# Written-out step loops, and attention's output sent to its rows from ScalarE's queue

## The reference

```python
q = (x @ wq).reshape(b, n, H, DH).transpose(0, 2, 1, 3)      # k and v alike; n = 1024, H = 16, DH = 16
sim = jnp.einsum('bhid,bhjd->bhij', _fq(q, dq, 128.0, 8), _fq(k, dk, 128.0, 8)) * SCALE
attn = jax.nn.softmax(sim, axis=-1)
out = jnp.einsum('bhij,bhjd->bhid', _fq(attn, dw, 0.0, 8), _fq(v, dv, 128.0, 8))
out = out.transpose(0, 2, 1, 3).reshape(b, n, D)
return out @ wo + bo
```

## Time and profile before

| | us |
|---|---|
| three runs | 2564.44, 2571.34, 2571.38 |
| median | 2571.34 |
| the profiled execution | 2566.87 |
| its span, first to last instruction | 2565.1 |
| busy: PE, DVE, ACT, POOL | 1997.6, 1810.0, 1136.4, 935.8 |
| ScalarE enters the loops' iterations | 13 times, first 328.2, last 2064.4: 144.7 apart |
| ScalarE waits for OS's matmuls (33 times) | 57.5 |
| VectorE's Pn waits for the transposes PT<-Pn (60 times) | 76.6 |
| TensorE waits for oT<-OS (13 times) | 16.1 |

### The profile page before, as it was taken

The page is one execution under the profiler, slowest core; times in us unless marked ns, Lnnn a source line. Parts: engine busy times, 40 slices in busy tenths (PEclk is TensorE's granted clock), DMA queues, the critical chain, the costliest instruction groups (busy, mean ns, idle before and its releaser), DMA issues.

```text
span 2565.1 us, 41654 instructions
## 1 busy us (share of the span) xinstructions
PE 1997.6 (78%) x10552; PEld 1431.5 (56%) x10552; DVE 1810.0 (71%) x3327; ACT 1136.4 (44%) x1906; POOL 935.8 (36%) x1629
## 2 busy tenths in 40 slices
PE   3665587878887887878888887879787887878786
PEld 3323265656665565656665565646565565656665
DVE  1566777696878777696877778686878778685632
ACT  1244535545454545545454545545353445444211
POOL 1213334343434334343434334343434334343212
PEclk8666698989999898989998898989888898989888
DMA  7486453634445353634445363634435353635010
GB/s 233 103 162 132 82 122 62 134 62 98 100 80 122 74 129 61 134 62 99 99 80 122 70 133 61 135 59 98 93 76 116 71 121 63 130 55 106 1 35 5
DMA packets 761579, 242.61 MB, mean 95 GB/s; under 512 B 675643, under 2 KB 757295, under 8 KB 761199
## 3 DMA queue, kind: packets, MB, share of 16 engines
q1 hardware_dynamic: 758127, 241.34, 45.0%
q10 hardware_dynamic: 3328, 0.01, 0.1%
HBM read 83.57 MB, written 19.25 MB: 40 GB/s over the span
## 4 chain that ended last, share of the span: by engine, by line
PE 46%; DVE 20%; issue 15%; ACT 7%; DMA 4%; SPq 4%; POOL 3%; DVEq 1%; ACTq 0%; POOLq 0%
PE work L1394 21%; PE work L1404 16%; ACT E L899 3%; PE rowps L1465 3%; DVE scaled_row L1055 3%; DVE Pn L1062 3%; DMA PT<-Pn 3%; PE outps L1450 2%; DVE hids L1202 2%; POOL scs L797 1%; DVE st L1078 1%; ACT hTs L875 1%; PE work L1387 1%; DVE xs L1192 1%; DVE scs L1216 1%
## 5 line engine op out<-in xcount | busy, mean ns | idle before, releaser
L1055 DVE TENSOR_SCALAR_CACHE_REDUCE scaled_row<-rowps,der 128x1024 uint8<-128x1024 f32 x512 | 654.8, 1279 | 359.1 <-PE rowps L1465 358.8
L899 ACT ACTIVATE E<-rowps,ebias,der 128x1024 f32<-128x1024 f32 x512 | 614.8, 1202 | 404.4 <-DVE scaled_row L1055 310.5
L1062 DVE TENSOR_SCALAR Pn<-E,rowinv 128x1024 int16<-128x1024 f32 x512 | 395.4, 772 | 113.0 <-DMA PT<-Pn 76.6
L731 POOL TENSOR_TENSOR rowden<-rowsum,raw 128x1 f32<-128x1 f32 x512 | 118.3, 231 | 948.7 <-ACT E L899 947.4
L1465 PE MATMUL rowps<-KC,QP 16*128 16x512 bf16 x1024 | 220.7, 428 | 212.4 <-ACT E L899 200.6
L734 POOL TENSOR_TENSOR rowinv<-rowden,minus 128x1 f32<-128x1 f32 x512 | 323.4, 632 | 91.4 <-POOL rowden L731 91.4
L1394 PE MATMUL work<-hTs,ff_w_sb 128*128 128x256 f32 x1024 | 259.5, 408 | 13.0 <-ACT hTs L875 13.0
L1465 PEld LDWEIGHTS rowps<-KC,QP 16*128 16x128 bf16 x1024 | 49.0, 92 | 379.9 <-ACT E L899 247.4
L1394 PEld LDWEIGHTS work<-hTs,ff_w_sb 128*128 128x128 f32 x1024 | 201.6, 203 | 59.0 <-issue 16.0
L1559 PE MATMUL work<-K,hids 128*128 128x154 f32 x1024 | 153.5, 301 | 35.0 <-DVE scs L1216 21.4
L1559 PEld LDWEIGHTS work<-K,hids 128*128 128x128 f32 x1024 | 137.2, 190 | 53.7 <-DVE scs L1216 27.8
(11 more groups left out here) (143 smaller groups left out, 3269.7 us busy)
## 6 DMA issues: line engine op xcount, KB each, us to landing
VW<-vw_dram SPq DMA_DIRECT2D x32, 640.0 KB, 4.8
KC<-k_dram SPq DMA_DIRECT2D x128, 64.0 KB, 2.3
VB<-v_dram SPq DMA_DIRECT2D x64, 128.0 KB, 3.1
PT<-Pn SPq DMA_TRANSPOSE x512, 3.1
V<-v_dram SPq DMA_DIRECT2D x16, 320.0 KB, 3.6
vw_dram<-scs SPq DMA_DIRECT2D x32, 154.0 KB
K<-k_dram SPq DMA_DIRECT2D x16, 308.0 KB, 3.3
K<-k_dram SPq DMA_DIRECT2D x32, 154.0 KB, 3.2
```

Source lines behind the costliest of these rows:

```text
L731: nc.gpsimd.tensor_tensor(rowden[:, n:n + 1], rowsum[:, n:n + 1], raw[:, DW1:DW1 + 1], ALU.mult).then_inc(row_den.sem, 1)
L899: nc.scalar.activation(E[:, slot, :], rowps[n % 2][:], ACT.Exp, bias=ebias[:, n:n + 1], scale=der[:, AL1:AL1 + 1], accum_out=rowsum[:, n:n ...
L1055: nc.vector.tensor_scalar(scaled_row[:, n % 2, :], rowps[n % 2][:], der[:, NAL1:NAL1 + 1], 3.0e38, ALU.mult, ALU.min, accum_out=ebias[:, n ...
L1062: nc.vector.tensor_scalar(Pn[:, n % 2, :], E[:, ring(n)[0], :], rowinv[:, n:n + 1], 255.0, ALU.mult, ALU.min).then_inc(row_round.sem, 1)
```

## The change

Two things. The loops over the steps become Python loops, so that all 18 steps are written out and the register instructions go. And ScalarE issues the four transfers of the output itself, right behind its copy to OS; it takes over the two waits that SyncE had there.

```diff
@@ all_steps
-                with eng.Fori(0, last - first) as i:
+                for i in range(last - first):
                     step(i + first, parts)
@@ attn_sync
-            def output(quad):
-                o_ready.wait(sp, v, quad + 1)
-                if quad == 0:
-                    l_filled.wait(sp, v - 1, 1)
-                for j in range(4):
-                    h = (4 * quad + j) % H
-                    sp.dma_start(oT[DH * (h % 8):DH * (h % 8) + DH, h // 8, :], OS[32 * j:32 * j + DH, :]
-                                 ).then_inc(o_out[j].sem, 16)
...
-                quad = (n - LAG - 9) // 8
-                if (n - LAG - 9) % 8 == 0 and (parts["old"] if quad < 0 else parts["attn"]):
-                    output(quad)
@@ attn_act, output
                 nc.scalar.activation(OS[:], outps[:, 0:CH], ACT.Copy, scale=der[:, OSC1:OSC1 + 1]).then_inc(o_ready.sem, 1)
+                o_ready.wait(act, v, quad + 1)
+                if quad == 0:
+                    l_filled.wait(act, v - 1, 1)
+                for j in range(4):
+                    h = (4 * quad + j) % H
+                    act.dma_start(oT[DH * (h % 8):DH * (h % 8) + DH, h // 8, :], OS[32 * j:32 * j + DH, :]
+                                  ).then_inc(o_out[j].sem, 16)
```

## The result

The changed kernel took 2611.64 us, the median of four runs (2607.75 to 2614.27), beside 2567.89 for the kernel before (2560.46 to 2571.38, four runs). The ratio is 1.0165 with a 95% interval of 1.0139 to 1.0191: 43.7 us slower. The profiled execution took 2612.05 (span 2610.2), in the middle of its runs.

What follows compares the result with a forecast made beforehand. It took no single engine as the bound, but a relay of TensorE, VectorE and ScalarE. Place 3's +35 and +4, 0 and 0 elsewhere, and -5 for the loops made +34: 2605 us on the median, range 2560 to 2640.

Steps and rivals of the forecast that it cites:

- the likeliest case: At place 3 four issues on ScalarE delay hTs, Wq waits and the clock falls: +34, 2605 us, chance 0.42.
- place 3: Attention's output for heads 12 to 15 of the unit before, at n = 5 of a step: +35 and +4.
- Rival A: At place 3 TensorE stands 3.35 us but its clock does not fall: +15, 2586 us, chance 0.21.
- Rival B: Four issues on ScalarE take 3.83 us instead of 2.55, also overrunning place 1's margin: +70, 2641 us, chance 0.12.
- Rivals C and D: C: register instructions on the path, place 3 free, 2535, chance 0.11. D: no change, issues 0.45 each, 2578, chance 0.14.
- place 3, ten steps, delay of hTs: Steps 2 to 11, with the pre chain: hTs 2.66 us late, 1.05 of it slack, row 1.6 late: +16.
- place 3, ten steps, clock: Steps 2 to 11: after TensorE's 3.35 us stand, Wq's first 8 matmuls run at 1.2 GHz, adding 1.9 a step.
- place 3, five steps without pre: Steps 12 to 16: hTs 2.26 us late, scores row read 0.86 late, clock already lower: +4.
- places 0 to 2: Output of heads 0 to 11: delay fits in slack, by 0.15 us at place 1, more at the others: cost 0.
- steps 0 and 1: Seven places, both queues tight: taken as 0, bounds a gain of 17 or a loss of 18 us.
- SyncE relieved: 4 x 2.45 us leave SyncE's queue per step; output lands earlier, but TensorE then waits for VectorE: gain 0.
- loops written out: 13 looped steps lose their register instructions, 0.4 us a step: 5 us gained.

Runs made afterwards that it cites:

- with the clock held: Changed kernel with six extra matmuls, result overwritten, filling TensorE's stand before Wq at place 3 in steps with the pre chain: 2582.07 us, ratio 1.0074.
- the single issue: Kernel before with loops written out, ScalarE issuing one of the four output transfers at each place and SyncE three: 2573.84 us, ratio 1.0033.
- the kernel that issues in ScalarE's stand: Changed kernel, with ScalarE's four issues at place 3 moved behind the exponentials of rows 6 and 7: 2583.28 us, ratio 1.0062.

## Why the prediction was right, and where it wasn't

The forecast was 2605 in a range of 2560 to 2640, slower; measured are 2611.6. The mechanism of the likeliest case held: the four issues stand ahead of hTs at place 3, Wq waits and the clock falls. Rival A (the clock stays) is out: it fell in all ten steps. Rival B (slow issues) is out: 2.44 and 2.48 us where I looked, and 2.51 to 2.56 from the end of the copy to ScalarE's next item, where I took 2.55. Rivals C and D are out with the size of the loss.

| term | predicted | measured |
|---|---|---|
| place 3, ten steps, delay of hTs | +16 | +18 (row 7.40 against 5.58 with the clock held) |
| place 3, ten steps, clock | +19 | +20 (9.43 against 7.40; Wq's busy time 131.6 to 151.6) |
| place 3, five steps without pre | +4 | row 0.3 later behind the copy in the mean of four steps; whole stretch -2.5, below the grain |
| places 0 to 2 | 0 | 0 (0.9962 against 0.9968) |
| steps 0 and 1 | 0 | +2.8, below the grain |
| SyncE relieved | 0 | not separated |
| loops written out | -5 | -8 and -5 (0.9968, 0.9982) |
| sum | +34 | +43.7 (the whole; the rows above, read against the kernel before, don't add up to it) |

**Place 3.** At the row where I closed the account, the changed kernel is 9.43 - 5.58 = 3.85 us later than the kernel before, predicted 3.5. The mis-sized term of the prediction is the slack: "since 1.05 of the 2.66 was slack". I read it in step 7 of the kernel before, where VectorE stood 1.84 us for a transpose. With the clock held, hTs 2.66 late makes the row 7.40 - 5.58 = 1.82 late, so the slack was 0.8 in the mean. It also belongs to the kernel with loops: with them written out the row comes at 4.90 without the move, and against that the changed kernel is 4.53 late. 2.66 of the stand (3.45 - 0.79) and 1.96 of Wq (5.58 - 3.62) are 4.62, so next to nothing is hidden at this row.

With that the sum can be written as 10 x 4.53 + 4 x 0.3 = 46.5 for the move, less 6.5 for the loops, +40 beside a measured +43.7. But one row doesn't carry that account. At VectorE's next reading the changed kernel is 3.9 us later than the kernel before and 4.0 later than the written-out loops, so that the 0.7 between these two is nearly gone. And with the loops kept, where the row is 8.93 - 5.58 = 3.35 late, the same sum gives some 35 where 55 were measured. That +40 comes near is partly luck. What the profiles support is 3.9 us a step at place 3, 4 more than I had over ten steps. The 43.9 us of the whole ten steps leave 5 for the rest of the step, less than two executions of one kernel differ by there. So the slack explains some 4 of the 10 us that the forecast was short; the rest stays open.

**Clock.** Predicted 1.9 us a stand, from a stand of 3.29 us elsewhere in the step; measured 1.96. A range of sizes lies behind the mean: Wq took 5.1 to 5.3 us in six of the ten steps and 6.06 in four, against 3.62. And the split was not as I said: Wq's first eight matmuls took 3.3 us in the mean and not 3.8, and the next eight were slowed too. That the total came out so near is partly luck.

**Places 0 to 2.** At place 1 I had 0.15 us of margin and expected it to hold. It held by at least 0.17: the exponential ends at 1195.59 and the row starts at 1195.90, 0.14 of it latency, behind the matmuls on Wup.

**Steps 12 to 16.** In step 13 the row comes 10.80 us after the copy's start and 9.98 before, 0.82 late against 0.86 predicted; it is 0.6 late in step 12, 0.2 early in step 14 and 0.2 late in step 15. Step 16 has no scores row left, so I should have counted four steps. That nothing shows in the sum over those steps is no contradiction: two executions of one kernel differ by 11.7 us there.

**Signs.** Most that I named as signs came: 2.44 us of issues, a stand of 3.42, no wait for the transpose ahead of the turned queries, no new row wait at place 1. The 3.8 us for Wq's first eight matmuls did not. The step length came out longer than said: 149.4 us from place 0 to place 0 in the mean of steps 2 to 10, where I had 147.5 to 148 and the kernel before has 144.5.

The Trainium skill says in "DMA: Bandwidth & Descriptors", section "Issuing engines are not separate DMA queues", that issuing elsewhere saves only sequencer time, which is usually small. For the gain this agrees: at places 0 to 2 the move changed nothing (0.9962 against 0.9968 and 0.9982). It says nothing of what stands behind an issue in its queue, and there 0.61 us an issue, four of them at place 3, cost 49 us.

**What stays open.** Four issues from ScalarE at place 3 that delay neither hTs nor, in one of the two kernels, anything of ScalarE's still cost 14 and 22 us; later transposes explain 5 to 6 of them. And the clock's falls in the rest of the step: in the profiles they hold the single issue's 8 us and most of the 13 us that the loops' writing-out is worth with ScalarE's issues (5 to 8 without them), but nothing here shows what sets them off.

## What to carry to other kernels

Before an issue is moved to a compute engine, look up what stands behind it in that engine's queue at each place and who waits for that: the same 2.5 us cost nothing at three places and 4.6 us a step at the fourth, and moving them behind one instruction gave back 35 of 49 us. Slack that is read from a profile belongs to the program as it is; where one part of a change removes the wait that made the slack, another part can't spend it. Follow a delay past the first row that shows it, too: 0.7 us late at one row was 0.3 at the next, and 2.5 us (the changed kernel with its stand filled, against the written-out loops) was 1.4 seven rows on. And a stand of TensorE can cost much again behind it in slower matmuls (here 1.6 us behind one of 2.14, 2.0 behind one of 3.45): if it can't be removed, matmuls whose result is thrown away can be worth their place.

## What the runs showed of the hardware

TensorE's granted clock fell behind shorter stands than I had thought. Before the same sixteen matmuls of Wq, with the same work ahead of them, it stayed behind stands of 0.79 and 1.50 us in every one of ten steps and had fallen behind 2.14 and 3.45 in every one. The price hardly depended on the stand: 1.64 us behind 2.14, 1.96 behind 3.45.

An issue can be slow by the time at which it is made, whatever it issues. In the stretch about 4.7 us behind place 3, while loads (VB, KC, VW) are under way, four output transfers took SyncE 3.87 us (2.4 at place 0); with them issued by ScalarE 2.8 us earlier, one transpose in the same place took 3.80, where the usual time is 1.23. In that kernel the first transpose issued there took over 2 us in nine of the ten steps. The output's own transfers were in flight then, so the loads alone are not shown to be the reason.

```profile
L533 SPq DMA_TRANSPOSE PT<-Pn x512: 1231/1233/4322, 92.1 to 2367.4; - x171
```

(All transposes of the kernel that issues in ScalarE's stand: min/median/max ns of an issue, first and last start.) So of the 3.87 us that the output took of SyncE's queue there, relieving it gave back only 1.4 in step 6 (the transpose's issue ended 8.5 us behind the copy, 9.9 before).
